# Row sums taken inside the value products, and one head group in four exponentiated after its transpose

## The reference

```python
scores = einsum('bhnqd,bhnkd->bhnqk', qw, kw) * scale + pos_bias   # 16 heads of 16, windows of 128
probs = softmax(scores, axis=-1)
ow = einsum('bhnqk,bhnkd->bhnqd', probs, vw)                       # added where windows overlap
h = h + (merged / counts) @ Wo + bo
h = h + experts(layernorm(h))                                      # top 2 of 8 experts, SwiGLU
```

## Time and profile before

| | us |
|---|---|
| median of three runs | 1357.6 (1352.97 to 1358.94) |
| the profiled execution, its own time | 1365.91 |
| its span, first to last instruction | 1364.1 |
| mean granted TensorE clock, share of full | 0.925 |
| busy: TensorE, VectorE, ScalarE, GpSimd | 1180.1, 913.4, 779.0, 571.8 |

### The profile page before, as it was taken

How to read it: one execution, slowest core, us unless ns; L and a number is a source line. 1 busy time by engine, 2 the same in 40 slices (tenths; PEclk the granted TensorE clock), 3 DMA queues, 4 the chain that set the end, 5 groups by cost and what they waited for, 6 DMA issues and landing times.

```text
span 1364.1 us, 34942 instructions
## 1 busy us (share of the span) xinstructions
PE 1180.1 (87%) x10190; PEld 949.8 (70%) x10191; DVE 913.4 (67%) x4211; ACT 779.0 (57%) x3176; POOL 571.8 (42%) x718
## 2 busy tenths in 40 slices
PE   1376889988998899889888764999999999999996
PEld 1254566666665666566666543999999999999995
DVE  4484998998989998999897754444444444444442
ACT  0295998999999999999999951111111111111110
POOL 5432466456545654565455332322223322222322
PEclk9687999888989898898889975999999999999998
DMA  3793564356436643664366126233233333333232
GB/s 113 150 238 84 117 149 90 89 129 145 85 90 137 136 92 92 137 131 89 93 125 133 33 68 184 40 48 50 46 48 48 46 47 50 46 46 50 46 47 31
DMA packets 98400, 123.35 MB, mean 90 GB/s; under 512 B 15544, under 2 KB 87416, under 8 KB 95192
## 3 DMA queue, kind: packets, MB, share of 16 engines
q1 hardware_dynamic: 75880, 89.96, 29.9%
q0 software_dynamic: 18576, 24.47, 11.2%
q10 hardware_dynamic: 3808, 7.34, 2.0%
HBM read 69.35 MB, written 46.07 MB: 85 GB/s over the span
## 4 chain that ended last, share of the span: by engine, by line
PE 67%; ACT 13%; issue 7%; DVE 4%; DMA 4%; POOL 1%; SPq 1%; ACTq 0%; DVEq 0%; another core or an unknown queue 0%; POOLq 0%
PE s_bank L1178 12%; PE t_bank L1178 12%; PE o_bank L1193 11%; ACT probs L628 10%; PE t_bank L1050 8%; PE m_bank L1114 5%; PE o_bank L1073 5%; PE s_bank L1036 4%; PE m_bank L1021 3%; PE m_bank L1014 3%; DMA qk_parts<-parts_flat 2%; DVE probs L765 2%; PE o_bank L1082 2%; ACT probsT L642 2%; PE m_bank L1167 1%
## 5 line engine op out<-in xcount | busy, mean ns | idle before, releaser
L628 ACT ACTIVATE probs<-probs,neg_max 128x128 f32<-128x128 f32 x1280 | 498.1, 403 | 7.5 <-issue 3.7
L765 DVE CUSTOM_DVE_ANT_0 probs<-s_bank,nbias 128x128 f32<-128x128 f32 x1280 | 291.8, 284 | 35.9 <-PE s_bank L1036 33.9
L628 ACT ACTIVATION_READ_ACCUMULATOR probs<-probs,neg_max 128x1 f32 x1280 | 260.4, 203 | 0.0
L1050 PE MATMUL t_bank<-ident,probs 128*128 128x128 f32 x1280 | 220.6, 300 | 39.6 <-ACT probs L628 39.2
L687 ACT ACTIVATE v_all<-s_bank 128x512 f32<-128x512 f32 x91 | 54.4, 598 | 287.7 <-PE s_bank L1178 267.8
L1050 PEld LDWEIGHTS t_bank<-ident,probs 128*128 128x128 f32 x1280 | 150.8, 154 | 54.0 <-ACT probs L628 50.9
L1036 PE MATMUL s_bank<-stacks 96*128 96x128 bf16 x1280 | 137.4, 234 | 49.4 <-DMA stacks<-qk_parts 32.3
L1193 PE MATMUL o_bank<-stacks,v_all 128*128 x728 | 172.7, 380 | 1.4 <-issue 1.2
L642 ACT ACTIVATE probsT<-t_bank 128x512 f32<-128x512 f32 x240 | 141.9, 591 | 51.1 <-PE t_bank L1050 49.7
L1036 PEld LDWEIGHTS s_bank<-stacks 96*128 96x128 bf16 x1280 | 94.2, 105 | 110.5 <-issue 39.1
L1073 PE MATMUL o_bank<-probsT,v_all 128*32 128x128 f32 x2560 | 146.0, 303 | 19.0 <-ACT probsT L642 12.6
(11 more groups left out here) (158 smaller groups left out, 2023.8 us busy)
## 6 DMA issues: line engine op xcount, KB each, us to landing
stacks<-qk_parts SPq DMA_DIRECT2D x192, 166.5 KB
qk_parts<-parts_flat SPq DMA_DIRECT2D x192, 83.2 KB
nbias<-expert_slots SPq DMA_DIRECT2D x91, 129.0 KB
w_sb<-in_L_ffn_w_dram ACTq DMA_DIRECT2D x14, 512.0 KB
v_all<-v_all SPq DMA_DIRECT2D x64, 96.0 KB, 3.2
x_here<-in_x_dram SPq DMA_DIRECT2D x16, 256.0 KB, 3.0
out_dram<-h_res SPq DMA_DIRECT2D x16, 256.0 KB
stacks<-in_L_ffn_w_dram SPq DMA_DIRECT2D x8, 512.0 KB
```

The lines of the kernel that those rows point to most:

```text
L628: ins = act.activation(seg, seg, ACT.Exp, bias=neg_max[:, r, i:i + 1], scale=-1.0, accum_out=row_sum[:, (par + v) % 2, h:h + 1])
L765: ins = dve.tensor_tensor_reduce(probs[:, r, i * WIN:(i + 1) * WIN], s_bank[:, k % 2, i * WIN:(i + 1) * WIN], nbias[:, h, :], 1.0, BIG, AL ...
L1050: mm = pe.transpose(t_bank[:, (k - 3) % 2, i * WIN:(i + 1) * WIN], probs[:, r, i * WIN:(i + 1) * WIN], ident[:, :])
```

## The change

The zeros between the value columns become ones, so that the value product gives each head's 16 outputs and its row sum. Each group then has its own 128 columns of `o_bank`. The exponentials no longer take a row sum. Per window ScalarE copies all 512 columns to `raw`, TensorE transposes the four blocks back, VectorE takes reciprocals and multiplies into `ctx_q`, TensorE transposes that, and ScalarE copies it to `head_out`. All probsT copies are ScalarE's now. For group LATE_G = 2 the four exponentials are left out: TensorE transposes the biased scores and subtracts the extreme by a product of `neg_max`, repeated over 128 columns, with `minus` (the negative unit matrix), and the copy from the bank is itself the exponential. The image's add and clamp go from VectorE to GpSimd, the h_res add waits for the first norm, and several steps move. Prefix counts and gate use columns of `m_bank` that were free.

```diff
+LATE_G = 2
...
+pool.memset(v_all[:, :], 1.0).then_inc(zeroed, 1)
...
+        if inp and k == 6:
+            pool.wait_ge(conv_step, b2 * 3 + 2)
+            pool.tensor_tensor(diag[:, :, :], diag[:, :, :], anti[:, :, :], ALU.add).then_inc(conv_step, 1)
+            pool.wait_ge(conv_step, b2 * 3 + 3)
+            if b2 >= 2:
+                pool.wait_ge(res_ready, b2 - 1)
+                pool.wait_ge(xn_ready, b2 * 3 - 3)
+            pool.tensor_scalar(h_in[par][:, 0:2, :], diag[:, :, :], 1.0, 0.0, ALU.min, ALU.max)\
+                .then_inc(image_ready, 1)
...
+            if inp:
+                pool.wait_ge(xn_ready, b2 * 3 + 3)
...
-        if (k >= 1 and att) or (k < 1 and tail):
-            g, r, v = (k - 1) % NG, (k - 1) % 4, (k - 1) // NG
+        if (k - 1) % NG != LATE_G and ((k >= 1 and att) or (k < 1 and tail)):
+            r = (k - 1) % 4
             act.wait_ge(max_ready, b * G + k)
-            if g == 0 and b * NW + v >= 2:
-                act.wait_ge(inv_ready, b * NW + v - 1)
-            for i, h in enumerate(group_heads(g)):
+            for i in range(GH):
                 seg = probs[:, r, i * WIN:(i + 1) * WIN]
-                ins = act.activation(seg, seg, ACT.Exp, bias=neg_max[:, r, i:i + 1], scale=-1.0,
-                                     accum_out=row_sum[:, (par + v) % 2, h:h + 1])
+                ins = act.activation(seg, seg, ACT.Exp, bias=neg_max[:, r, i:i + 1], scale=-1.0)
             ins.then_inc(exp_ready, 1)
...
-        if g != 3 and ((k >= 2 and att) or (k < 2 and tail)):
+        if (k >= 2 and att) or (k < 2 and tail):
             n = b * G + (k - 2)
             act.wait_ge(pT_done, n + 1)
             if n >= 2:
                 act.wait_ge(pv_done, n - 1)
-            act.activation(probsT[:, k % 2, :], t_bank[:, k % 2, :], ACT.Copy).then_inc(pT_by_act, 1)
+            if g == LATE_G:
+                ins = act.activation(probsT[:, k % 2, :], t_bank[:, k % 2, :], ACT.Exp, scale=-1.0)
+            else:
+                ins = act.activation(probsT[:, k % 2, :], t_bank[:, k % 2, :], ACT.Copy)
+            ins.then_inc(pT_ready, 1)
         v = (k - 4) // NG
         if (k - 4) % NG == 3 and ((att and v >= 0) or (tail and v < 0)):
-            act.wait_ge(weightT_done, b * NW + v + 1)
-            if b * NW + v >= 1:
-                act.wait_ge(head_ready, b * NW + v)
-            act.activation(weightT[:, :], o_bank[:, (par + v) % 2, C * WIN:2 * C * WIN], ACT.Copy)\
-                .then_inc(weightT_ready, 1)
+            wv = b * NW + v
+            act.wait_ge(pv_done, wv * NG + NG)
+            if wv >= 1:
+                act.wait_ge(rawT_done, wv)
+            act.activation(raw[:, :], o_bank[:, (par + v) % 2, :], ACT.Copy).then_inc(raw_ready, 1)
+        v = (k - 7) // NG
+        if (k - 7) % NG == 3 and ((att and v >= 0) or (tail and v < 0)):
+            wv, vp = b * NW + v, (par + v) % 2
+            act.wait_ge(headT_done, wv + 1)
+            if wv >= 2:
+                act.wait_ge(ctx_added, wv - 1)
+            act.activation(head_out[:, vp, :], o_bank[:, vp, 0:C * WIN], ACT.Copy).then_inc(head_ready, 1)
...
-        v = (k - 2) // NG
-        if (k - 2) % NG == 3 and ((att and v >= 0) or (tail and v < 0)):
-            n, wv, vp = b * G + (k - 2), b * NW + v, (par + v) % 2
-            dve.wait_ge(exp_ready, n + 1)
+        v = (k - 6) // NG
+        if (k - 6) % NG == 3 and ((att and v >= 0) or (tail and v < 0)):
+            wv, vp = b * NW + v, (par + v) % 2
+            rows_q = o_bank[:, vp, :].rearrange("p (u n) -> p u n", u=2)
+            inv = inv_sum[:, vp, :].rearrange("p (u i a) -> p u i a", u=2, a=2)
+            sums = [rows_q[:, :, a * WIN:(a + 1) * WIN].rearrange("p u (i e) -> p u i e", i=GH)
+                    [:, :, :, (1 - a) * HD:(1 - a) * HD + 1] for a in range(2)]
+            dve.wait_ge(rawT_done, wv + 1)
             if wv >= 2:
-                dve.wait_ge(weight_ready, wv - 1)
-            dve.reciprocal(inv_sum[:, vp, :], row_sum[:, vp, :]).then_inc(inv_ready, 1)
-            dve.wait_ge(pT_done, n + 1)
-            if n >= 2:
-                dve.wait_ge(pv_done, n - 1)
-            dve.tensor_copy(probsT[:, k % 2, :], t_bank[:, k % 2, :]).then_inc(pT_by_dve, 1)
-            dve.wait_ge(inv_ready, wv + 1)
-            if wv >= 2:
-                dve.wait_ge(weightT_done, wv - 1)
-            dve.tensor_reduce(weight[:, vp, :, :],
-                              inv_sum[:, vp, :].unsqueeze(2).unsqueeze(3).to_broadcast([P, H, HD, 1]),
-                              AX.X, ALU.add)\
-                .then_inc(weight_ready, 1)
-        v = (k - 5) // NG
-        if (k - 5) % NG == 3 and ((att and v >= 0) or (tail and v < 0)):
-            wv, vp = b * NW + v, (par + v) % 2
-            dve.wait_ge(weightT_ready, wv + 1)
-            if wv >= 2:
-                dve.wait_ge(ctx_added, wv - 1)
-            dve.tensor_tensor(head_out[:, vp, :], o_bank[:, vp, 0:C * WIN], weightT[:, :], ALU.mult)\
-                .then_inc(head_ready, 1)
+                dve.wait_ge(ctx_q_ready, wv * 2 - 2)
+            for a in range(2):
+                dve.reciprocal(inv[:, :, :, a:a + 1], sums[a]).then_inc(inv_ready, 1)
+            if wv >= 1:
+                dve.wait_ge(headT_done, wv)
+            heads = ctx_q[:, :].rearrange("p (u i a e) -> p u i a e", u=2, i=GH, a=2)
+            for a in range(2):
+                dve.wait_ge(inv_ready, wv * 2 + 1 + a)
+                src = rows_q[:, :, a * WIN:(a + 1) * WIN].rearrange("p u (i e) -> p u i e", i=GH)
+                dve.tensor_tensor(heads[:, :, :, a, :], src[:, :, :, a * HD:(a + 1) * HD],
+                                  inv[:, :, :, a:a + 1].to_broadcast([P, 2, GH, HD]), ALU.mult)\
+                    .then_inc(ctx_q_ready, 1)
...
             n, r = b * G + (k - 3), (k - 3) % 4
-            pe.wait_ge(exp_ready, n + 1)
+            g, w = (k - 3) % NG, b * NW + (k - 3) // NG
+            if g == LATE_G:
+                pe.wait_ge(max_ready, n + 1)
+            else:
+                pe.wait_ge(exp_ready, w * (NG - 1) + g + (1 if g < LATE_G else 0))
             if n >= 2:
-                if (k - 5) % NG == 3:
-                    pe.wait_ge(pT_by_dve, b * NW + (k - 5) // NG + 1)
-                else:
-                    pe.wait_ge(pT_by_act, (b * NW + (k - 5) // NG) * 3 + (k - 5) % NG + 1)
+                pe.wait_ge(pT_ready, n - 1)
             for i in range(GH):
-                mm = pe.transpose(t_bank[:, (k - 3) % 2, i * WIN:(i + 1) * WIN],
-                                  probs[:, r, i * WIN:(i + 1) * WIN], ident[:, :])
+                seg = t_bank[:, (k - 3) % 2, i * WIN:(i + 1) * WIN]
+                mm = pe.transpose(seg, probs[:, r, i * WIN:(i + 1) * WIN], ident[:, :])
+                if g == LATE_G:
+                    mm = pe.matmul(seg, neg_max[:, r, i:i + 1].to_broadcast([P, WIN]), minus[:, :],
+                                   start=False, stop=True, skip_group_check=True)
             mm.then_inc(pT_done, 1)
...
-                mm = pe.matmul(o_bank[32 * i:32 * i + 32, vp, (g // 2) * WIN:(g // 2 + 1) * WIN],
+                mm = pe.matmul(o_bank[32 * i:32 * i + 32, vp, g * WIN:(g + 1) * WIN],
                                v_win[bp][:, w, c0:c0 + 2 * HD],
                                probsT[:, (k - 4) % 2, i * WIN:(i + 1) * WIN],
-                               start=(g % 2 == 0), stop=(g % 2 == 1), skip_group_check=True)
+                               start=True, stop=True, skip_group_check=True)
             mm.then_inc(pv_done, 1)
-            if g == 3:
-                pe.wait_ge(weight_ready, b * NW + m // NG + 1)
-                for c in range(C):
-                    mm = pe.transpose(o_bank[:, vp, (C + c) * WIN:(C + c + 1) * WIN],
-                                      weight[:, vp, 8 * c:8 * c + 8, :].rearrange("p h d -> p (h d)"),
-                                      ident[:, :])
-                mm.then_inc(weightT_done, 1)
+        v = (k - 5) // NG
+        if (k - 5) % NG == 3 and ((att and v >= 0) or (tail and v < 0)):
+            wv, vp = b * NW + v, (par + v) % 2
+            pe.wait_ge(raw_ready, wv + 1)
+            for g in range(NG):
+                mm = pe.transpose(o_bank[:, vp, g * WIN:(g + 1) * WIN], raw[:, g * WIN:(g + 1) * WIN],
+                                  ident[:, :])
+            mm.then_inc(rawT_done, 1)
+        v = (k - 7) // NG
+        if (k - 7) % NG == 3 and ((att and v >= 0) or (tail and v < 0)):
+            wv, vp = b * NW + v, (par + v) % 2
+            pe.wait_ge(ctx_q_ready, wv * 2 + 2)
+            for c in range(C):
+                mm = pe.transpose(o_bank[:, vp, c * WIN:(c + 1) * WIN], ctx_q[:, c * P:(c + 1) * P],
+                                  ident[:, :])
+            mm.then_inc(headT_done, 1)
...
-        if tail2 and k == 2:
-            counted = o_bank[:, par, :]
+        if tail2 and k == 1:
             pe.wait_ge(taken_ready, b9 + 1)
```

(38 more changed lines are left out.)

76 lines of the change are left out of this document (34 added, 42 removed).

## The result

| | before | after |
|---|---|---|
| median (lowest to highest), us | 1357.53 (1352.97 to 1358.94), 4 runs | 1423.26 (1422.56 to 1427.76), 4 runs |
| ratio, 95% interval | 1 | 1.0497 (1.0464 to 1.053) |
| profiled execution: own time, span | 1365.91, 1364.1 | 1422.93, 1421.1 |
| mean granted TensorE clock | 0.925 | 0.969 |

The account below looks back on a forecast made before the run. ScalarE bounds the kernel at 45.7 us an image; then TensorE does, its floor 43.95 plus waits 6.05 plus 0.5 making 50.5. That is 4.75 more over fourteen images, 66 us on 1357.6: 1424 us, range 1335 to 1475.

Parts of the forecast that it names:

- ScalarE falls to 33.9, VectorE below 38: Image stage: ScalarE's work falls nine us an image to 33.9, exponentials costing 0.29 each; VectorE's falls below 38 us.
- TensorE's floor rises from 36.75 to 43.95: TensorE's work per image without waits: late-group products 0.90 and raw transposes 0.54, five times an image, add 7.2 us.
- The raw wait, 0.89 five times: TensorE stands before the raw transposes until ScalarE's copy to `raw`: 0.89 us, five times, 4.4 us an image.
- The prefix behind xT, 1.0: TensorE's prefix product at step 1 waits for xT, copied behind the late bank's exponential: 1.0 us an image.
- exp(9) behind copy(7), 0.5: In the window without projections, step 9's exponentials stand behind step 7's copy: 0.5 us an image.
- v, 0.15: TensorE's v projection waits behind the later h2: 0.15 us an image.
- The 0.5 for ScalarE's stand: ScalarE's 2 us stand once an image now lands on TensorE, partly covered by other waits: 0.5 us added.
- half clock hides behind ScalarE: TensorE's half-clock stretches are hidden behind ScalarE before the change; a share moving over a few us an image refutes the forecast.
- (1) Covered waits: Rival: TensorE's new waits are covered and only its floor is left, 1332 us; chance 0.11.
- (2) TensorE has room: Rival: only TensorE's weight loads count, so ScalarE sets a period of 38.4 us, 1255 us; chance 0.04.
- (3) Half clock on the path: Rival: ten us an image stay at half clock, some 5 us more TensorE work shows, 1494 us; chance 0.09.
- (4) and (5): Rivals: half the waits covered, period 46.5 to 48.5, 1368 to 1396 us, 0.13; saving and waits cancel within 0.5%, 0.05.

Follow-up runs that it names:

- the doubling experiment: The changed kernel with each late-group product with `minus` issued twice, eight more records a window: 1493.61 us, ratio 1.1167.
- the sets at 1336: The unchanged kernel before, run again in two later sets of runs: medians 1337.2 and 1335.5 us.
- the first experiment: The changed kernel with its four raw transposes issued one step later, behind the late group's transposes: 1358.74 us, ratio 1.016.
- the version with VectorE's copy: Changed kernel with raw transposes and prefix later, no late group, and each window's last probsT copy on VectorE: 1337.16 us, then 1338.06 us.

## Why the prediction was right

- **ScalarE bound the kernel before.** Relieved of row sums alone it lost 27 us, so ScalarE was on the path; part of that may be the clock, which rose with it.
- **ScalarE falls to 33.9, VectorE below 38.** Measured 35.5 and 36.1. The exponential at 0.29 was right. The xn operation did not return to 0.41; it takes 0.70 to 0.74. Off the path, as said.
- **TensorE's floor rises from 36.75 to 43.95.** The rows give 44.4, and the doubling experiment shows that added work on it is paid. The late group costs 0.89 (0.90 foreseen).
- **The raw wait, 0.89 five times.** It is 0.90 in two windows of five and 0.64 in three, where 0.20 for `head_out`, a wait that the sum didn't have, stands ahead of it. Taking it away gave 4.3 us an image, for 4.4 foreseen. This step carried the forecast: without it the kernel is at 1359.
- **The prefix behind xT, 1.0.** From start to start 1.11 (419.90 + 0.35 to 421.36), and 1.0 by its removal alone. **exp(9) behind copy(7), 0.5**: 4.8 us in ten images, 0.48, in two places of each image. **v, 0.15**: 0.17 (445.49 + 0.35 to 446.01).
- **The 0.5 for ScalarE's stand was wrong.** In ten images no wait of TensorE is above 1.04 us, where one of 1.70 stood before; waits of 1.5 us and more stood there in four images of ten, not in each. The remaining terms make 50.0 and the profile has 49.8. Against 45.7 that is 4.1 an image and not 4.75.
- **That half clock hides behind ScalarE was not borne out.** The prediction named as a sign of being wrong that its share moves by more than a few us an image. It did: at 0.91 about 8 us of an image of 45.7 were at half clock, and after the change none. The forecast had no term for that. The period after, 50.5 against 49.8, stands without it, being built from TensorE's starts at full clock. But what it is compared with, 45.7 and 1357.6, had the half clock in it, by the spread of the kernel before some 3 us an image (8 times 0.4, an estimate). At full clock the loss by work and waits would be nearer to 7 us an image than to 4.
- **So part of the closeness is luck.** Thirteen images at 4.0 are 52 us of the 57 by which the spans differ. The forecast added 66 to 1357.6, and the medians do differ by 65.7, because the profiled execution of before was itself 8 us above its median. Against the sets at 1336 the same kernel is 6.6% slower, not 5.0.

The rivals. **(1) Covered waits** fell with the first experiment: removing one of them gave 66 us. **(2) TensorE has room** fell with the doubled product: forty more records cost all of their 4.46 us. Its source was the rule of the Trainium skill, "Perfetto Trace Analysis", Identifying the Most-Contended Engine, that TensorE's headroom is judged by MFU (the share of peak arithmetic, not worked out here) and the busy share of the weight loads; here weight loads were busy 67% of a stretch in which added work was paid one for one. What measured headroom was the distance from one start to the next. **(3) Half clock on the path** fell too: the granted clock was 1.00 over the ten images after, and over those with the doubled product. The forecast had named in favour of this rival the Trainium skill, "TensorE: Matmul & The Clock Gate", Part 4, by which a transpose "doesn't count as PE-busy the same way"; with more transposes than before the rows show full clock throughout, which doesn't separate transposes from the products among them. Half clock did come onto the path in one variant, the one without a late group, at 0.94. Of **(4) and (5)** nothing is left at a period of 49.8.

What the forecast did not look for is that the change's two halves work on each other. The late group costs TensorE 0.89 a window and shortens its wait for `raw` by 0.64. That is a small loss; by the account above it was a gain of 23 us only because the longer waits came with half clock. With the raw transposes a step later neither the wait nor the half clock is there, and the loss shows: 30 us.

Left open: whether the clock makes the kernel before move by 2% between sets or only moves with it; what ScalarE does in its long stands of 1.4 to 2.5 us; and why waits of 1.61 us came with half clock in one kernel while one of 1.55 an image didn't in another (the version with VectorE's copy, 1.00).

## What to carry to other kernels

When work is moved from one full engine to another, first make the receiver's floor by counting starts where nothing was waited for, then add each new round trip at its place in both queues. Here the waits were 5.9 of the 13 us that TensorE's period rose above its old floor, and moving one block of four transposes by one step gave back 66 us. Test the parts of a change alone and again after the largest wait is gone: the same edit was worth 23 us at first and cost 30 afterwards. When a variant comes out against the sum, split its period into busy and idle time and look at the granted clock before naming a wait: the same instructions took 2.7 us more of busy TensorE in one image than in the next. Added work on an engine that is 89% busy can be paid in full.

## What the runs showed of the hardware

- A 128 x 128 exponential costs 0.39 us from start to start with its row sum and 0.29 without (0.295 in the kernel before with only that removed). The accumulator's read isn't hidden.
- TensorE's granted clock was 0.91 over ten images before, and 1.00 in the image stage of every version with less work on ScalarE but one: without a late group and with raw waits of up to 1.61 us it was 0.94. There TensorE's four raw transposes took 0.91 us to the next start (417.21 to 418.12) instead of 0.49.
- A small VectorE operation can become six times longer beside one of GpSimd. The same instruction, 128 x 16, over the same ten images before and after:

```profile
L812 DVE TENSOR_SCALAR onehot<-onehot,text_ok 128x16 f32<-128x16 f32 x10 | 2.3, 235 | 0.4
```

```profile
L835 DVE TENSOR_SCALAR onehot<-onehot,text_ok 128x16 f32<-128x16 f32 x10 | 14.2, 1417 | 0.4
```

  The timeline of the kernel after at one of these, VectorE and GpSimd:

```profile
467.36 1.71 DVE L835 TENSOR_SCALAR onehot<-onehot,text_ok 128x16 f32<-128x16 f32 x1
467.93 1.10 POOL L547 TENSOR_TENSOR diag<-x_here,x_below 128x512 f32<-128x512 f32 x1
```

  It ends 0.04 us after GpSimd's first pass over an incoming image, a pass that the kernel before has too. In the eleven traces of kernels with the change, 116 operations on `onehot` take over 1 us; each runs beside this pass and ends within 0.05 us of its end. No operation on `onehot` without this pass beside it is above 0.66 us in any of the fourteen traces. Before, the two never met. The change moved them together, and where a variant moved them by a step's part, the operation ahead (L829, 1.84 us above) was the long one. No run moved the pass alone.
